# First norm of block i+2 moved into the feed-forward stage, with the order of SyncE, GpSimd and the maxima transposes changed

## The reference

```python
def layernorm(x):                      # no scale; layer_norm(x, g, b) of the FFN has one
    return (x - mean(x)) / sqrt(var(x) + 1e-5)

def xattn(q, k, v, Wq, Wk, Wv, Wo, lam, g):     # k = v = ctx, 154 rows; 16 heads of 32, 8 KV heads
    q1, q2 = split(q @ Wq.T, 2); k1, k2 = split(k @ Wk.T, 2); vh = v @ Wv.T
    w = softmax(q1 @ k1.T) - lam * softmax(q2 @ k2.T)      # per head, over the 154 rows
    attn = (w @ vh)                                        # heads side by side: 512 columns
    attn = attn * rsqrt(mean(attn**2) + 1e-5) * g * (1 - LAMBDA_INIT)
    return attn @ Wo.T

def ffn(x, ...):
    h = layer_norm(x, ln1_g, ln1_b) @ ternary(w1).T + b1   # 512 -> 2048
    h = layer_norm(gelu(h), ln2_g, ln2_b)
    return h @ ternary(w2).T + b2                          # 2048 -> 512

# x: (4, 2048, 512) fp32, ctx: (4, 154, 512) fp32
x = x + xattn(layernorm(x), ctx, ctx, ...)
x = x + ffn(layernorm(x), ...)
```

## Time and profile before

| | us |
|---|---|
| median of three runs | 2472.6 |
| profiled execution | 2467.48 |
| span of its trace | 2465.1 |
| TensorE busy (13663 matmuls) | 2301.0 (93%) |
| VectorE busy | 1744.0 (71%) |
| ScalarE busy | 1342.8 (54%) |
| GpSimd busy | 1008.1 (41%) |

### The profile page before, as it was taken

One profiled execution on the slowest core, in us unless ns is written; L12 is line 12 of the kernel. 1 busy time (PEld: TensorE's weight loads), 2 busy tenths in 40 slices (PEclk: granted clock), 3 DMA queues, 4 the chain that ended last, 5 costly groups with the idle time before them and its releaser, 6 DMA issues.

```text
span 2465.1 us, 35548 instructions
## 1 busy us (share of the span) xinstructions
PE 2301.0 (93%) x13663; PEld 1080.5 (44%) x13663; DVE 1744.0 (71%) x2714; ACT 1342.8 (54%) x1943; POOL 1008.1 (41%) x823
## 2 busy tenths in 40 slices
PE   8478999999999999999999999999999999999978
PEld 5243444535354443535344453534435353544433
DVE  3875858677686868768586776858587785857673
ACT  3325555546555555556555555655555565555544
POOL 0220533626153452716244271625436162534517
PEclk9688999999999999999999999999999999999999
DMA  7230203021130302021030202103030210302000
GB/s 257 72 81 7 69 15 91 15 65 28 40 79 15 90 15 73 19 64 40 23 96 15 80 12 69 36 23 82 15 101 15 68 27 24 81 15 73 15 22 17
DMA packets 105643, 125.85 MB, mean 51 GB/s; under 512 B 22496, under 2 KB 74268, under 8 KB 104964
## 3 DMA queue, kind: packets, MB, share of 16 engines
q1 hardware_dynamic: 105476, 123.60, 17.6%
HBM read 51.80 MB, written 20.36 MB: 29 GB/s over the span
## 4 chain that ended last, share of the span: by engine, by line
PE 67%; DVE 21%; issue 4%; ACT 3%; POOL 3%; DMA 2%; SPq 0%; POOLq 0%; DVEq 0%; ACTq 0%
PE ps L1325 16%; PE ps L1347 7%; PE ps L1337 5%; PE ps L1272 5%; PE ps L1173 5%; PE ps L1225 5%; PE ps L1250 4%; PE ps L1279 4%; PE ps L1174 4%; PE ps L1175 4%; DVE attn_raw L928 2%; DVE arena L987 2%; DVE arena L890 2%; DVE arena L951 2%; PE ps L1255 2%
## 5 line engine op out<-in xcount | busy, mean ns | idle before, releaser
L526 POOL TENSOR_TENSOR attn_raw<-attn_raw 128x512 f32<-128x512 f32 x448 | 580.8, 1315 | 145.7 <-ACT attn_raw L685 137.8
L1325 PE MATMUL ps<-rows,w1T 128*128 128x512 f16 x2048 | 484.1, 379 | 3.3 <-DVE rows L982 3.3
L890 DVE TENSOR_REDUCE arena<-ps 128x3 f32<-128x462 f32 (+1 forms) x704 | 413.4, 618 | 96.4 <-PE ps L1225 94.9
L494 POOL TENSOR_TENSOR q<-q 128x512 f16<-128x512 f32 x128 | 151.3, 1182 | 680.8 <-ACT q L631 679.3
L680 ACT ACTIVATE attn_raw<-ps,vec_cols,wstep 128x512 f32<-128x512 f32 x256 | 198.6, 776 | 251.6 <-PE ps L1325 249.7
L987 DVE SCALAR_TENSOR_TENSOR arena<-attn_raw,vec_cols,arena 128x512 f16<-128x512 f32 x256 | 233.6, 913 | 83.1 <-ACT arena L683 81.5
L651 ACT ACTIVATE arena<-ps 128x1024 f32<-128x1024 f32 x128 | 131.6, 1028 | 280.1 <-PE ps L1250 280.1
L1325 PEld LDWEIGHTS ps<-rows,w1T 128*128 128x128 f16 x2048 | 190.6, 97 | 197.5 <-DVE rows L982 15.2
L1347 PE MATMUL ps<-w2T,arena 128*128 128x512 f16 x1088 | 271.1, 379 | 0.0
L910 DVE SCALAR_TENSOR_TENSOR p<-arena,p 128x512 f16<-128x512 f32 x128 | 88.1, 689 | 245.2 <-ACT p L655 245.2
L1225 PE MATMUL ps<-k_att,stack_raw 96*128 96x154 f16 x2048 | 222.9, 233 | 23.4 <-DVE arena L890 22.6
(11 more groups left out here) (164 smaller groups left out, 3468.5 us busy)
## 6 DMA issues: line engine op xcount, KB each, us to landing
stack_raw<-q SPq DMA_DIRECT2D x768, 64.0 KB, 2.0
arena<-in_x SPq DMA_DIRECT2D x16, 1024.0 KB, 6.3
arena<-in_x SPq DMA_DIRECT2D x64, 256.0 KB, 2.7
out<-arena SPq DMA_DIRECT2D x64, 256.0 KB, 2.0
arena<-in_L_ffn_w SPq DMA_DIRECT2D x8, 1024.0 KB, 10.4
stack_raw<-in_L_xattn_Wq SPq DMA_DIRECT2D x8, 256.0 KB, 10.8
k_att<-k_store SPq DMA_DIRECT2D x4, 490.0 KB
k_store<-attn_raw SPq DMA_DIRECT2D x12, 160.0 KB
```

The lines of the kernel that those rows point to most:

```text
L526: ins = pool.tensor_tensor(acc[:, e, :], acc[:, e, :], src[:, j % NG, :], ALU.add)
L890: dve.tensor_reduce(negmax[:, tt, u0:u1], ps[:, row_bank(c, tb), 0:(u1 - u0) * S].rearrange("p (u s) -> p u s", s=S), AX.X, ALU.max, negat ...
L1325: ins = pe.matmul(ps[:, B_H + j % 2, :], w1T[:, k, j * P:(j + 1) * P], rows16[:, e, k, :], start=(k == 0 and e == 0), stop=(k == KD - 1 an ...
```

## The change

- **First norm of block i+2.** Its statistics leave the place ahead of `mid_rows` and are taken one tile at a time in steps 1 to 4 of the feed-forward stretch, ahead of `gelu_lo`; aggregation and variance follow in step 4 (`ln1_variances`). GpSimd's power stands ahead of the sum of step 5. The rows are normalised behind `gelu_lo` in steps 6 and 7, two each. The transposes of x move from steps 8 and 10 to 9 and 11.
- **`MAXIMA_AT`.** The 44 pieces are spread otherwise: two each in steps 0 to 4 and 6 (before 1, 2, 2, 3, 3 and 3), two in 11, four in 12 to 14.
- **SyncE.** The query pairs 0 and 1 are stacked ahead of the loads of keys and x; the pairs 2 and 3 stay behind them.
- **GpSimd.** The four additions of the constant all precede the power of the second norm of the feed-forward layer (before: one ahead, three behind). The low halves of queries 5 to 7 wait until the four rows of `mid_rows` are normalised. 
- **Maxima transposes.** They leave the end of iteration i and stand behind the first eight `ffn_late` matmuls of iteration i+1.

Lines of the changed kernel are numbered four higher from VectorE's block on (`L861` is `L865`, `L876` `L880`, `L890` `L894`, `L987` `L991`), and seven higher on TensorE (`L1232` is `L1239`).

```diff
--- before.py
+++ after.py
@@ -69,7 +69,8 @@
 QATT, QEARLY = 4, 7
 FLAG = 3
 NG = 3
-XT_AT = {8: (0, 1), 10: (2, 3)}
+LN1_STATS_AT, LN1_AT, LN1_ROWS_AT = {1: (0,), 2: (1,), 3: (2,), 4: (3,)}, 4, {6: (0, 1), 7: (2, 3)}
+XT_AT = {9: (0, 1), 11: (2, 3)}
 WFIRST = 13
 
 PROLOGUE = [(w.rstrip("0123456789"), int(w.lstrip("tqmrxys") or 0)) for w in (
@@ -77,7 +78,7 @@
     "q3 t30 t31 q4 ys r0 m0 yr q5 m1 q6 q7 yt m2 m3").split()]
 MSHARE = [range(0, 8), range(8, 20), range(20, 32), range(32, NT)]
 WCHUNK = 4
-MAXIMA_AT = (1, 2, 2) + (3,) * (JH - 3)
+MAXIMA_AT = (2, 2, 2, 2, 2, 3, 2, 3, 3, 3, 3, 2, 4, 4, 4, 3)
 TLAST = JH - 1
 PAIR = 2 * UPT
 QDMA = 3 * UPT * 16
@@ -444,6 +445,9 @@
                         store(i - 1, tt)
                         load_x_res(i, tt - 1)
                     load_x_res(i, TT - 1)
+                if i + 1 < NBLK:
+                    for p in range(QATT // 2):
+                        stack_queries(i + 1, p, i)
                 if i + 1 < NBLK and (i + 1) % BLK_PER_BATCH == 0:
                     load_keys((i + 1) // BLK_PER_BATCH)
                 if i + 2 < NBLK:
@@ -451,7 +455,7 @@
                 if i + 1 < NBLK and (i + 1) % BLK_PER_BATCH == 0:
                     load_values((i + 1) // BLK_PER_BATCH)
                 if i + 1 < NBLK:
-                    for p in range(QM // 2):
+                    for p in range(QATT // 2, QM // 2):
                         stack_queries(i + 1, p, i)
                     stack_maxima(i + 1)
 
@@ -530,24 +534,24 @@
                 ahead, ahead2 = i < NBLK - 1, i < NBLK - 2
                 for what, n in ATTEND:
                     if what == "g" and i:
-                        add_constant(i - 1, (0,))
+                        add_constant(i - 1, range(TT))
                         power(3, s_gln, s_rstd4, i - 1)
-                        add_constant(i - 1, range(1, TT))
                     elif what == "a":
                         sum_squares(i, n)
                     elif what == "q" and ahead:
                         q_lo(i + 1, n)
                 power(1, s_var2, s_rstd2, i)
-                if ahead2:
-                    power(0, s_var1, s_rstd1, i + 2)
                 power_half(i, 0)
                 if ahead:
                     q_lo(i + 1, QATT)
                 power_half(i, 1)
+                wait(pool, s_xhat2, i, TT, TT)
                 if ahead:
                     for n in range(QATT + 1, QM):
                         q_lo(i + 1, n)
                 for j in range(JH):
+                    if ahead2 and j == LN1_AT + 1:
+                        power(0, s_var1, s_rstd1, i + 2)
                     if j:
                         sum_gelu(i, j)
 
@@ -855,13 +859,13 @@
                 dve.scalar_tensor_tensor(out_const[:], ps[:, 2, :], wstep[:, 1:2], out_const[:], ALU.mult,
                                          ALU.add).then_inc(s_rows, 1)
 
-            def ln1_stats(c):
+            def ln1_stats(c, tts=range(TT)):
                 wait(dve, s_xin, c, 16, 16)
-                for tt in range(TT):
-                    ins = dve.bn_stats(stats[:, 0, tt, :], x_in[:, tt, :])
-                ins.then_inc(s_st1, 1)
-
-                wait(dve, s_st1, c, 1, 1)
+                for tt in tts:
+                    dve.bn_stats(stats[:, 0, tt, :], x_in[:, tt, :]).then_inc(s_st1, 1)
+
+            def ln1_variances(c):
+                wait(dve, s_st1, c, TT, TT)
                 dve.memset(gate[:], 0.0)
                 for tt in range(TT):
                     ins = dve.bn_aggr(mv[:, 0, tt, :], stats[:, 0, tt, :])
@@ -869,10 +873,10 @@
                 wait(dve, s_ag1, c, 1, 1)
                 dve.tensor_scalar(var[:, 0, :], mv[:, 0, :, 1], EPS, None, ALU.add).then_inc(s_var1, 1)
 
-            def ln1_rows(c):
+            def ln1_rows(c, tts=range(TT)):
 
                 wait(dve, s_rstd1, c, 1, 1)
-                for tt in range(TT):
+                for tt in tts:
                     dve.tensor_scalar(x_in[:, tt, :], x_in[:, tt, :], mv[:, 0, tt, 0:1], rstd[:, 0, tt:tt + 1],
                                       ALU.subtract, ALU.mult).then_inc(s_xhat1, 1)
 
@@ -1035,17 +1039,19 @@
                         add_ffn(i - 1, n, ffn_bank(n))
                     elif what == "z" and i:
                         add_shift(i - 1, n)
-                if ahead2:
-                    ln1_stats(i + 2)
                 mid_rows(i)
-                if ahead2:
-                    ln1_rows(i + 2)
                 h_lo(i)
                 for j in range(JH):
                     beside = maxima_beside(j) if ahead else []
                     for tb in beside[:2]:
                         row_max(i + 1, tb)
+                    if ahead2 and j in LN1_STATS_AT:
+                        ln1_stats(i + 2, LN1_STATS_AT[j])
+                    if ahead2 and j == LN1_AT:
+                        ln1_variances(i + 2)
                     gelu_lo(i, j)
+                    if ahead2 and j in LN1_ROWS_AT:
+                        ln1_rows(i + 2, LN1_ROWS_AT[j])
                     for tb in beside[2:]:
                         row_max(i + 1, tb)
                     if ahead2 and j in XT_AT:
@@ -1061,6 +1067,7 @@
                     ternary(n)
                 elif what in ("xs", "ys"):
                     ln1_stats(0 if what == "xs" else 1)
+                    ln1_variances(0 if what == "xs" else 1)
                 elif what in ("xr", "yr"):
                     ln1_rows(0 if what == "xr" else 1)
                 elif what in ("xt", "yt"):
@@ -1366,8 +1373,10 @@
                         scores(i, n)
                     elif what == "v":
                         values(i, n)
-                    elif what == "e" and i:
-                        ffn_late(i - 1, n, range(JH // 4))
+                    elif what == "e":
+                        if i:
+                            ffn_late(i - 1, n, range(JH // 4))
+                            transpose_maxima(i)
                     elif what == "f" and i:
                         ffn_late(i - 1, n, range(JH // 4, JH))
                     elif what == "h" and i:
@@ -1408,8 +1417,6 @@
                         x_transposes(i + 2, XT_AT[j])
                 for j in range(JH - FLAG, JH):
                     ffn_step(i, j, banks)
-                if ahead:
-                    transpose_maxima(i + 1)
 
             setup()
             for what, n in PROLOGUE:
```

## The result

| us | before | after |
|---|---|---|
| median of four runs each, same chip | 2473.3 | 2488.6 (2487.7 to 2493.5) |
| ratio, 95% interval | | 1.0062 (1.0046 to 1.0078) |
| span of the profiled execution | 2465.1 | 2485.3 |
| ordinary block | 141.58 | 143.48 |

The change makes the kernel slower, by 15.3 us of the medians. Forecast were 2482 us, 9.6 more, and a slower kernel as the likeliest case. The two profiled executions stand 20.2 us apart.

The account below looks back on a forecast made before the run. The prediction took TensorE, busy 93% of the span, as the bound. Turn -25.5, middle -14.6, every fourth block -6.3 and feed-forward +56 sum to +9.6 us on 2472.6, giving 2482 us, range 2434 to 2512.

Parts of the forecast that it names:

- Turn: From late matmuls to the next block's first scores: scores start 1.7 us sooner, 15 times, -25.5 us.
- the power as the last to come: In the turn, GpSimd's power ends at about 1472.1, after the four additions; scores follow at 1474.2.
- Middle: Around `mid_rows`: `L670` 0.7 us sooner and `L982` no longer 0.3 us late, 1.0 us 14 times; -14.6 in all.
- the queries no longer run beside `L976`: In the middle: transposed rows ready at about 1407.8 instead of 1409.3, since queries 5 and 6 run elsewhere.
- The 0.6 us for the block without a norm: In the middle of the block that has no `L876`: a gain of 0.6 us, once.
- Every fourth block: Three blocks that load new keys: their waits for x and stacked queries go, -6.3 us.
- the late load of keys: Keys issued 15 us later must be there for first row scores: no loss taken, bound 0 to 2 us three times.
- Feed-forward: Feed-forward stretch: added VectorE work held by GpSimd makes TensorE wait, about 4.0 us per block, 14 times, +56 us.
- the walk: Step-by-step feed-forward working: TensorE waits 1.8, about 2.0 and 1.4 us for pieces 12, 17 and 19, 5.2 per block.
- The forecast's sign of being wrong: In feed-forward steps 5 to 8: VectorE's `gelu_lo` taking 0.75 us would show the forecast wrong.
- The cause named: In the feed-forward stretch: VectorE instructions wait for GpSimd's running sum to end, held 0.4 to 1.27 us.
- rival 3: Feed-forward: longer holding, GpSimd falls behind too, 7 us per block, +52, 2524 us; chance 0.13 together with another rival.

Follow-up runs that it names:

- e1: Kernel before plus the turn's two edits alone (all four additions ahead of GpSimd's power, maxima transposes moved): 2446.1 us, ratio 0.989.
- e10: Kernel before with only the maxima transposes moved behind the first eight late matmuls, GpSimd's additions left: 2455.0 us, ratio 0.992.
- e11: Changed kernel without GpSimd's wait for the normalised rows of `mid_rows`: 2493.7 us, ratio 1.008 to the kernel before.
- e5: Kernel before plus the turn's edits and GpSimd's wait for the normalised rows, first norm in its old place: 2444.6 us, ratio 0.988.
- e3: Changed kernel with GpSimd's GELU sums on 8 of 512 columns: 2416.2 us, one run.
- e4: Kernel before with GpSimd's GELU sums on 8 of 512 columns, as a control: 2445.3 us, one run.
- e9: Changed kernel plus eight matmuls filling TensorE's wait in step 7: 2494.4 us, ratio 1.0085 to the kernel before.
- e2: Changed kernel with the turn as before and without GpSimd's wait for the normalised rows: 2534.2 us, ratio 1.024 to the kernel before.
- e8: Changed kernel with the first norm's row instructions on 8 of 512 columns: 2447.9 us, one run.
- e6: Changed kernel with the first norm placed mostly where GpSimd has no sums, x loaded and maxima spread otherwise: 2436.2 us, ratio 0.984 to before.

## Why the prediction was right, and where it was not

**Turn, -1.7 forecast:** -1.73 in block 8, -1.8 in e1. The working held at each step, the power as the last to come included, and the two edits add up as 1.17 and 0.64 (e10, e1).

**Middle, -1.0:** -1.13, `L674` right behind the table's dummy. But the reason "the queries no longer run beside `L976`" is not it: e11 shows that the wait brings nothing, since the rows are done early enough without it. What brings the 1.1 us is the move of the norm: the stretch is 77.48 us in e5, with the turn and the wait and the norm in its old place, and 76.34 in e11. The traces tell the two parts apart. The rows of x keep `L982` back: in e5 it starts when they end, though `L670` is in time. The statistics keep `mid_rows` back: without them its rows start 69.91 us into the stretch instead of 70.46, and in e11 they are done before the table load is over, held or not. The 0.6 us for the block without a norm were nothing: block 14 took 76.35 us in the kernel before already.

**Every fourth block, -6.3:** right; all three excesses are gone but for the late fall of the clock in one, and the late load of keys costs nothing. Which of the causes, SyncE's order or the later place of the norm, does it was not told apart.

**Feed-forward, +4.0:** +4.9 in block 8, the term that was mis-sized; 0.9 us, 14 times, is 13 us. By the starts of `hidden`, steps 5, 7 and 8 take 3.99, 5.47 and 5.63 us where an unheld one takes 3.20 (e3), so they lose 0.8, 2.3 and 2.4 us, 5.5 together where the walk has 1.8, 2.0 and 1.4, together 5.2. (An idle time as a row shows it is some 0.2 us less than what the step loses.) That these sums lie so close is partly luck. The first was walked too long, because `gelu_lo` of steps 4 and 5 met no sum; the two behind the rows too short by 1.3 us. The forecast's sign of being wrong, a `gelu_lo` of 0.75 us in steps 5 to 8, is there in steps 5 and 7 and not in 6 and 8; it is the held rows that cost the time. The larger part of the miss is in the last steps: beside the two more pieces (0.4 us), which the walk has, the steps with four pieces wait 0.6 us where it has 0.2 in all. That part has nothing to do with holding, as e3 and e4 show. The cause named, the holding of VectorE by GpSimd's sums, is shown for 3.6 of the 4.9 us by the same pair.

**Not in the prediction:** the clock. It costs little here, 1.6 us in one block of 13 and nothing where the next wait covers it (e9). It costs much in e2, where eleven blocks have the late fall.

The Trainium skill's page "SBUF — State Buffer", section "Who interferes with whom", also has GpSimd blocked for a whole VectorE instruction. The prediction read next to nothing of that from its rows, but this trace agrees with the page. In the kernel after:

```profile
1437.10 1.26 POOL L530 TENSOR_TENSOR attn_raw<-attn_raw 128x512 f32<-128x512 f32 x1
...
1440.06 0.74 DVE L991 SCALAR_TENSOR_TENSOR arena<-attn_raw,vec_cols,arena 128x512 f16<-128x512 f32 x1
1440.13 1.79 POOL L530 TENSOR_TENSOR attn_raw<-attn_raw 128x512 f32<-128x512 f32 x1
```

The first sum begins beside maxima and statistics and takes 1.26 us; the second begins 0.07 us behind a `gelu_lo` and takes 0.53 longer. In blocks 1 to 13 the 192 sums that begin while a `gelu_lo` is under way take 1.31 to 1.80 us, 1.48 as the median, and those that begin with VectorE idle 1.26 to 1.27. What failed is the price: a sum is put off by 0.05 to 0.5 us and not by 0.7, the mean of all grew only from 1315 to 1380 ns, and the period by 1.9 us, not by the 4.3 (7 less 1.7 and 1.0) that the loss of rival 3 would make. For the VectorE side e8 agrees with the page, whatever the length: 1.23 us for an instruction of 8 columns.

In sum: 14 x 4.9 = 69, less 15 x 1.8 = 27, less 14 x 1.13 = 16, less 6.3, plus 1.6, is +21 us, against 20.2 between the two spans and 15.3 between the medians. So by the spans the change costs twice the 9.6 forecast. By the medians it costs less, as the profiled execution of before lies 5.8 us under its median and that of after 0.9 under its own; that helped the forecast by luck.

## What to carry to other kernels

An engine's idle time in a stretch is no room for more work while a neighbour can hold it: ask of each instruction that is added whether the other engine has one running when it arrives, since it costs the rest of that one beside its own length. Put such work where the neighbour is silent (e6), and test the cause with a control that has the same edit on the kernel before (e4), or what the other parts of the change cost is put down to the cause. And before a slow instruction is called a cost, look at what the next wait does without it (e9): what is covered comes back as waiting.

## What the runs showed of the hardware

- Behind a wait of 2.1 us, in a stretch in which TensorE was otherwise busy (22.07 of 24.80 us), the granted clock fell to 0.50 and was back within 5 us. In 13 blocks of the same program it did so behind the first such wait in ten, behind the second in one and not at all in two; filling the first kept it at 1.00 in eleven of 13.
- The holding goes both ways: VectorE's `gelu_lo` took 1.29 to 1.80 us instead of 0.74 behind the start of a GpSimd sum, and a sum up to 1.79 us instead of 1.26 behind the start of a `gelu_lo`.
- Two full rows of x, one behind the other on VectorE, each wait for a sum of their own (2.89 us for the pair), as GpSimd's next instruction gets in first; two rows of 8 columns do so once (1.43 us).
- Batch statistics (0.68 us per tile) and maxima (0.62 us) beside GpSimd's sums take no longer than without.
